# Reading the FFN weights earlier: absolute sums in the QKV stage, quantisation in the attention stage

## The chip, the cores and the metric

The kernel runs on all 8 cores of one Trainium2 chip. Each core computes one of the 8 sequences by itself and holds its own copy of the weights in device memory; the cores exchange nothing. The metric is device microseconds (us) of the slowest core.

## The reference

One transformer layer on `x` of shape (8, 4096, 1024), float32: `x = x + Attn(LN(x))`, then `x = x + FFN(LN(x))`. LN has no gain or bias.

```python
# attention, one head, d_k = 128, causal
Q, K, V = x @ Wq, x @ Wk, x @ Wv
attn = softmax(mask(Q @ K.T * 128 ** -0.5)); out = (attn @ V) @ Wo
# FFN, 1024 -> 4096 -> 1024, weights and activations quantised
def _weight_quant(w):
    scale = 1.0 / clip(mean(abs(w)), 1e-05)
    return clip(round(w * scale), -1.0, 1.0) / scale
def _act_quant(x):
    scale = 127.0 / clip(max(abs(x), axis=-1), 1e-05)
    return clip(round(x * scale), -128.0, 127.0) / scale
gate = silu(_act_quant(x) @ wq(w_gate).T); up = _act_quant(x) @ wq(w_up).T
y = _act_quant(gate * up) @ wq(w_down).T
```

What matters here is `_weight_quant`: each of the three 16 MB weight matrices needs the mean of its absolute values before a single element can be quantised. So each matrix is read from memory twice: pass 1 sums the absolute values, pass 2 multiplies by the scale, clips, rounds and stores bf16.

## The kernel before

The program is written out by hand as five instruction lists, one an engine, with explicit semaphores. `sc.op(engine, fn, waits, inc)` appends an instruction to the list of TensorE ('t'), VectorE ('v'), ScalarE ('s'), GpSimd ('g') or SyncE ('q'). Nothing reorders them later: each engine works through its list in the order in which the Python code emitted it, and an instruction that waits holds all that stand behind it. A DMA is an instruction of the engine that issues it ('q' and 'g' for loads, 's' for most stores).

The 4096 rows of `x` are NT = 32 tiles of 128 rows. The stages follow one another:

1. **QKV stage** (`emit_p1_A`, `emit_p1_B`, `emit_p1_geo`). Per tile: load x into one half of `x2_st` (named x_st in the profile; two buffers), DVE sums the rows (L234), ACT squares and sums them (L239), a chain of small DVE instructions and one ACT Sqrt (L254) give mean and 1/sigma, ACT normalises into `nqh_sb[:, 0:1024]` (L261), PE transposes, DVE copies, PE makes Q, K and V, DVE and ACT evict them (L294, L296, L298). On each engine the sum and the square of tile i+1 are emitted ahead of the rest of tile i; the x load of tile i+2 waits for L261 of tile i.
2. **Attention stage** (`emit_pa1_group`), 8 groups g of 4 query tiles. PE computes scores (L479), ACT takes the exponential (L490 to L497), PE multiplies by V (L454), DVE inverts the row sums (L516), ACT scales the output (L522) and stores it (L527). After each group **pass 1** of the weights follows: four pieces of 128x2048 of w_gate or w_up and four of 128x1024 of w_down (`emit_w1_piece`). A piece is a load (L206) and an ACT Abs with a running sum (L210). Each kind of piece has two buffers: `x2_st` and `wstage` for the wide ones, loaded by SP, `nqh_sb` and `nqt_sb` for the narrow ones, loaded by POOL. `emit_scales` follows the last group: for each of the three matrices a chain of small DVE and PE instructions (L320 to L339).
3. **Wo stage**, 8 groups of 4 tiles. Per group the attention output comes back (L575), PE transposes it, DVE copies it (L594). Per tile: PE multiplies by Wo (L632, L635), DVE adds x (L641, L643) in one of four x buffers (loaded at L430 into the two halves of `x2_st` and of `wstage`), ACT issues the store of x1 (L647), and one tile later the statistics of the second LN follow (`emit_stats`: DVE L604, ACT L609, DVE L613 to L619). The load of tile i+4 waits for statistics and store of tile i. Between the add and the statistics stands **pass 2**: one wide and one narrow piece per tile (`emit_w2_piece`). A piece is a load (L379), two DVE instructions (L382, L385) and one ACT instruction (L388 into the resident `wgq` or `wuq`; L395 into the single buffer `wdq_st`, which ACT then stores to memory, L397). Two buffers per kind: parts of `qres` and `kres`, free since attention is over, for the wide pieces, `nqh_sb` and `nqt_sb` for the narrow ones.
4. **FFN stage**: per tile the quantised activations times `wgq` and `wuq` (L790, L797), silu, product, quantisation.
5. **Down stage**: per tile the product with the quantised w_down (L936).

The two rules that bind a piece of pass 2 for w_down are in these lines: the buffer's next load waits for the ACT instruction, and the ACT instruction waits for the store before it.

```python
            if idx >= 33:
                wds.append(('DSW', ds_wdq[idx - 1]))
            s_qdone[idx] = sc.op('s', (lambda dstap=dstap: (lambda e: e.activation(
                wdq_st, dstap, AF.Identity, bias=ng_c)))(), waits=wds, inc='S')
```

## Time and profile before

| what | us |
|---|---|
| median of 2 runs | 2870.09 (2844.27 and 2895.91) |
| the profiled execution | 2851.59 |
| its span, slowest core (core 4) | 2850.0 |
| spans of the eight cores | 2828.4 to 2850.0 |
| QKV stage, to the first score matmul | 0 to 335.9 |
| attention stage with pass 1 | 335.9 to 646.3 |
| Wo stage with pass 2 | 646.3 to 1046.3 |
| FFN stage | 1046.3 to 2362.4 |
| down stage | 2362.4 to 2850.0 |

The span is the time from the first to the last instruction of the profiled execution; the execution's own time is 1.6 us longer. In the rows below PE is TensorE's matmul, PEld its weight load, DVE VectorE, ACT ScalarE, POOL GpSimd, SP SyncE; an engine's name with a q (ACTq, SPq) is its sequencer issuing a DMA. PEclk is TensorE's granted clock as a share of 2.4 GHz. "DMA share" is the mean busy share of the core's 16 DMA engines. Buffer numbers are left out of names.

### The profile page before, as it was taken

How to read it: one execution, taken by the hardware profiler on the slowest of the kernel's cores; microseconds unless marked ns; L12 is line 12 of the kernel's file. 1: busy time of each engine (PE TensorE's matmuls, PEld its weight loads, DVE VectorE, ACT ScalarE, POOL GpSimd, SP SyncE). 2: the span in 40 equal slices, each digit the busy share in tenths (PEclk: the TensorE clock that was granted, in tenths of full speed). 3: DMA queues.
4: the chain of work that ended last, by engine and by line, in shares of the span. 5: the costliest groups of instructions: out<-in, count | busy, mean ns of one | idle time of the engine just before them, and what ended most of it. 6: DMA issues, size and time to landing. Idle time of an engine off the chain costs nothing.

```text
span 2850.0 us, 25295 instructions; the slowest of 8 cores (2828.4 to 2850.0 us)
## 1 busy us (share of the span) xinstructions
PE 1692.4 (59%) x9479; PEld 881.7 (31%) x9618; DVE 912.1 (32%) x1481; ACT 866.0 (30%) x829; POOL 95.1 (3%) x168
## 2 busy tenths in 40 slices
PE   2333313330001017877777787778777875999999
PEld 2333212230000003333333333334333432444444
DVE  2333200004556554334434433443444331000110
ACT  2322355562333333333333333333333331000000
POOL 1000011011111100000000000000000000000000
PEclk9855556665555559999999999999999997999999
DMA  3111354446777740100110011001001006444443
GB/s 68 52 52 55 102 183 152 162 139 227 244 242 233 241 161 30 45 30 37 45 45 30 38 45 45 30 37 45 37 32 44 37 15 211 158 148 148 148 156 125
DMA packets 69993, 290.07 MB, mean 102 GB/s; under 512 B 10352, under 2 KB 12400, under 8 KB 53488
## 3 DMA queue, kind: packets, MB, share of 16 engines
q1 hardware_dynamic: 28592, 143.73, 15.8%
q0 software_dynamic: 21696, 68.17, 7.8%
q10 hardware_dynamic: 19584, 76.55, 6.6%
q8 instruction: 77, 1.26, 0.2%
q14 instruction: 44, 0.36, 0.0%
HBM read 212.93 MB, written 76.55 MB: 102 GB/s over the span
## 4 chain that ended last, share of the span: by engine, by line
PE 55%; DMA 13%; DVE 12%; ACT 9%; issue 8%; DVEq 1%; POOL 1%; ACTq 0%; SPq 0%; POOLq 0%
PE pb L797 17%; PE pb L790 16%; PE pb L936 16%; DMA nqt_sb<-wdt 4%; DMA nqh_sb<-wdt 4%; DVE h_sb L809 3%; ACT kres L807 3%; DMA wstage<-wgt 1%; ACT nqh_sb L261 1%; DVE st_cols L814 1%; DVE st_cols L234 1%; ACT wdq_st L395 1%; DMA wdqh<-wdq_st 1%; PE pb L274 1%; PE pb L283 1%
## 5 line engine op out<-in xcount | busy, mean ns | idle before, releaser
L790 PE MATMUL pb<-wgq,qres 128*128 128x512 bf16 x1952 | 770.7, 395 | 254.5 <-DVE qres L773 251.7
L797 PE MATMUL pb<-wuq,qres 128*128 128x512 bf16 x2048 | 806.2, 394 | 43.0 <-DVE h_sb L809 38.1
L936 PE MATMUL pb<-wdq_sb,nqt_in 128*128 128x512 bf16 x2007 | 442.1, 380 | 25.0 <-DMA nqt_in<-nqh 22.6
L809 DVE SCALAR_TENSOR_TENSOR h_sb<-pb,st_cols,kres 128x1024 f32<-128x1024 f32 x128 | 164.3, 1284 | 736.4 <-ACT kres L807 736.4
L790 PEld LDWEIGHTS pb<-wgq,qres 128*128 128x128 bf16 x2048 | 206.9, 101 | 551.2 <-issue 332.0
L807 ACT ACTIVATE kres<-pb,st_cols 128x1024 f32<-128x1024 f32 x128 | 142.5, 1113 | 495.6 <-PE pb L797 333.5
L797 PEld LDWEIGHTS pb<-wuq,qres 128*128 128x128 bf16 x2048 | 205.6, 100 | 253.3 <-issue 33.6
L936 PEld LDWEIGHTS pb<-wdq_sb,nqt_in 128*128 128x128 bf16 x2048 | 200.8, 98 | 266.0 <-issue 25.9
L632 PE MATMUL pb<-wo_sb,ot_sb 128*128 128x512 bf16 x30 | 18.1, 603 | 319.8 <-DVE ot_sb L594 319.8
L867 ACT ACTIVATE nqh_sb<-h_sb,konst 128x4096 bf16<-128x4096 f32 x32 | 118.7, 3708 | 215.1 <-DVE h_sb L865 215.1
L479 PE MATMUL pb<-qres,kres 128*128 128x128 bf16 x528 | 52.4, 260 | 189.0 <-ACT pt L497 174.3
L946 DVE SCALAR_TENSOR_TENSOR out_sb<-pb,c_all,x_in 128x512 f32<-128x512 f32 x32 | 24.0, 750 | 431.2 <-PE pb L936 431.2
L814 DVE TENSOR_REDUCE st_cols<-h_sb 128x1 f32<-128x1024 f32 x128 | 156.1, 1220 | 11.7
L274 PE MATMUL pb<-ident_sb,nqh_sb 128*128 128x128 bf16 x256 | 32.4, 306 | 184.9 <-ACT nqh_sb L261 184.9
L632 PEld LDWEIGHTS pb<-wo_sb,ot_sb 128*128 128x128 bf16 x32 | 4.1, 127 | 332.6 <-issue 332.6
L479 PEld LDWEIGHTS pb<-qres,kres 128*128 128x128 bf16 x528 | 42.1, 119 | 195.1 <-issue 192.5
L516 DVE RECIPROCAL rq_sb<-pb 128x1 f32<-128x1 f32 x32 | 2.9, 154 | 284.9 <-PE pb L454 284.9
L274 PEld LDWEIGHTS pb<-ident_sb,nqh_sb 128*128 128x128 bf16 x256 | 24.8, 137 | 192.3 <-issue 192.3
L865 DVE TENSOR_SCALAR h_sb<-h_sb,st_cols,konst 128x4096 f32<-128x4096 f32 x32 | 77.2, 2411 | 5.3 <-DVE c_all L863 5.3
L739 ACT ACTIVATE qres<-ln_scr,konst 128x1024 bf16<-128x1024 f32 x32 | 36.7, 1148 | 130.4 <-DVE ln_scr L732 130.4
L839 ACT ACTIVATE nqt_sb<-pb 128x2048 bf16<-128x2048 bf16 x31 | 58.2, 1877 | 21.1 <-PE pb L832 21.1
L497 ACT ACTIVATE pt<-pb,konst 128x1024 bf16<-128x1024 f32 x56 | 59.0, 1112 | 7.4 <-PE pb L479 4.5
(147 smaller groups left out, 1556.1 us busy)
## 6 DMA issues: line engine op xcount, KB each, us to landing
nqh<-nqt_sb ACTq DMA_DIRECT2D x32, 1024.0 KB, 3.9
nqt_in<-nqh SPq DMA_DIRECT2D x32, 1024.0 KB, 5.2
x_st<-x POOLq DMA_DIRECT2D x48, 512.0 KB, 4.6
nqh_sb<-wdt POOLq DMA_DIRECT2D x32, 512.0 KB, 7.3
nqt_sb<-wdt POOLq DMA_DIRECT2D x32, 512.0 KB, 7.4
x_st<-x1h SPq DMA_DIRECT2D x32, 512.0 KB, 3.3
x_in<-x1h SPq DMA_DIRECT2D x32, 512.0 KB, 6.8
y<-out_sb ACTq DMA_DIRECT2D x32, 512.0 KB, 7.0
```

Source lines behind the costliest of these rows:

```text
L274: tt = sc.op('t', (lambda c=c, par=par: (lambda e: e.transpose(psA[par][:, c * 128:(c + 1) * 128], ln1_sb[:, c * 128:(c + 1) * 128], ident ...
L479: tt = sc.op('t', (lambda k=k, q=q, pbst=pbst, off=off, j=j: (lambda e: e.matmul(pbst[:, off + j * 128: off + (j + 1) * 128], kres[:, k * ...
L497: s_exp_last[pp] = sc.op('s', (lambda pp=pp, ptx=ptx: (lambda e: e.activation(pt_row[ptx][:, 0:1024], pb[pp][:, 0:1024], AF.Exp, scale=sms ...
L790: tt = sc.op('t', (lambda c=c, o0=o0, gb=gb, half=half, par=par: (lambda e: e.matmul(gb[:, half * 512:(half + 1) * 512], xqTb[par][:, c * ...
L797: tt = sc.op('t', (lambda c=c, o0=o0, ub=ub, half=half, par=par: (lambda e: e.matmul(ub[:, half * 512:(half + 1) * 512], xqTb[par][:, c * ...
L807: s_silu_q[(i, qtr)] = sc.op('s', (lambda gb=gb, i=i: (lambda e: e.activation(g_s, gb, AF.Silu, scale=c1g_p[i % 2])))(), waits=sw, inc='S')
L809: v_stt_q[(i, qtr)] = sc.op('v', (lambda qtr=qtr, ub=ub, i=i: (lambda e: e.scalar_tensor_tensor(h_sb[:, qtr * 1024:(qtr + 1) * 1024], ub, ...
L814: sc.op('v', (lambda qtr=qtr: (lambda e: e.reduce_max(mh4[:, qtr:qtr + 1], h_sb[:, qtr * 1024:(qtr + 1) * 1024], axis=AX, apply_absolute_v ...
L839: ss2 = sc.op('s', (lambda fg=fg: (lambda e: e.activation(nqt_sb[:, 0:2048], fg.bitcast(BF16)[:, 0:2048], AF.Identity)))(), waits=sw2, inc ...
L865: vv = sc.op('v', lambda e: e.tensor_scalar(h_sb, h_sb, s2q_c, cb_c, ALU.mult, ALU.add), waits=[('V', v_stt_q[(i, 3)])], inc='V')
L867: s_nqh_t[i] = sc.op('s', lambda e: e.activation(nqh_sb, h_sb, AF.Identity, bias=ng_c), waits=[('V', vv)], inc='S')
L936: tt = sc.op('t', (lambda c=c, half=half, par=par: (lambda e: e.matmul(dps[par][:, half * 512:(half + 1) * 512], nqt_in[par][:, c * 128:(c ...
```

## The change

Both passes over the weights move one stage ahead.

- Pass 1 goes into the QKV stage: after each tile three pieces are emitted, 96 in all. All pieces are now 128x1024, all are loaded by SP, and they go through four buffers: the two halves of `wstage` and the columns 1024 to 3072 (bf16) of `nqh_sb` and `nqt_sb`, which the QKV stage does not use. The first four loads wait for nothing.
- `emit_scales` stands between the QKV stage and attention, and the first scores wait for it.
- Pass 2 goes into the attention stage: after each of the 8 groups eight pieces are emitted, the 32 wide ones of w_gate and w_up after groups 0 to 3, the 32 of w_down after groups 4 to 7. All are loaded by SP, through four buffers of 128x2048: `x2_st`, `wstage`, `nqh_sb`, `nqt_sb`.
- The Wo stage has no weight work left. Its first x loads wait for the last ACT instruction of pass 2 and for its store to memory.

```diff
-    w1stages = [x2_st, wst2]
+    w1stages = [wst2[:, 0:1024], wst2[:, 1024:2048],
+                nqh_sb.bitcast(F32)[:, 512:1536], nqt_sb.bitcast(F32)[:, 512:1536]]
+    w2stages = [x2_st, wst2,
+                nqh_sb.bitcast(F32)[:, 0:2048], nqt_sb.bitcast(F32)[:, 0:2048]]
...
     def emit_w1_piece(idx):
         wi, src, wid = wpieces[idx]
...
+        par = idx % 4
+        dstap = w1stages[par][:, 0:wid]
+        w = [('S', s_abs[idx - 4])] if idx >= 4 else []
+        v = sc.op('q', (lambda src=src, dstap=dstap: (lambda e: e.dma_start(out=dstap, in_=src)))(),
+                  waits=w, inc='DQW%d' % par, n=16)
...
     for i in range(NT):
         if i + 1 < NT:
             emit_p1_A(i + 1)
         s_ln1x = emit_p1_B(i)
         emit_p1_geo(i, s_ln1x)
+        for _ in range(3):
+            if w1_next < len(wpieces):
+                emit_w1_piece(w1_next)
+                w1_next += 1
...
     def emit_w2_piece(idx):
         wi, src, dst, wid = p2pieces[idx]
         s_col = wsc[:, 2 * wi:2 * wi + 1]
...
+        par = idx % 4
+        dstap = w2stages[par][:, 0:wid]
+        if idx < 4:
+            w = [('S', s_abs[-1]), ('T', p1_T), ('V', p1_V), ('S', s_lastx[NT - 1])]
         else:
...
+            w = [('S', s_qdone[idx - 4])]
+        v = sc.op('q', (lambda src=src, dstap=dstap: (lambda e: e.dma_start(out=dstap, in_=src)))(),
+                  waits=w, inc=w2sems[par], n=16)
...
     def emit_xload_pa(i):
...
-            w = [('S', s_abs[-1])]
+            w = [('S', s_qdone[-1] if s_qdone[-1] else 0), ds_wd_done]
...
+    emit_scales()
+    w2_next = 0
     for g in range(NT // GRP):
         emit_pa1_group(g)
-        for _ in range(4):
-            if w1_next < 32:
-                emit_w1_piece(w1_next)
-                w1_next += 1
...
-    emit_scales()
+        for _ in range(8):
+            if w2_next < len(p2pieces):
+                emit_w2_piece(w2_next)
+                w2_next += 1
...
             ds_x1[i] = ('DSX%d' % pari, v)
-            if w2_next[0] < 32:
-                emit_w2_piece(w2_next[0])
-                w2_next[0] += 1
-            if wd2_next[0] < 64:
-                emit_w2_piece(wd2_next[0])
-                wd2_next[0] += 1
             if j >= 1:
                 emit_stats(i - 1)
```

Line numbers shift: of the changed kernel L198 is the Abs (before L210), L227 the square (L239), L242 the Sqrt (L254), L249 the normalisation (L261), L284 the eviction of K (L296), L373 and L380 the ACT instruction of pass 2 (L388, L395), L382 its store (L397), L624 the store of x1 (L647), L586 the square of the second LN (L609).

ACT's list in the QKV stage, before, from the Sqrt of one tile to the Sqrt of the next (x2_st is the profile's x_st):

```order
L254 ACTIVATE st_cols<-st_cols,konst 128x1
L261 ACTIVATE nqh_sb<-x2_st,st_cols 128x1024
L296 ACTIVATE kres<-pb1 128x128
L239 ACTIVATE ln_scr,st_cols<-x2_st 128x1024
L254 ACTIVATE st_cols<-st_cols,konst 128x1
```

The same place in the changed kernel:

```order
L242 ACTIVATE st_cols<-st_cols,konst 128x1
L249 ACTIVATE nqh_sb<-x2_st,st_cols 128x1024
L284 ACTIVATE kres<-pb1 128x128
L198 ACTIVATE wstage0,wsums<-wstage0 128x1024 x2
L198 ACTIVATE nqh_sb,wsums<-nqh_sb 128x1024
L227 ACTIVATE ln_scr,st_cols<-x2_st 128x1024
L242 ACTIVATE st_cols<-st_cols,konst 128x1
```

Three Abs instructions (two halves of wstage, then nqh_sb) now stand between the eviction of K and the square of the tile after next, and so ahead of the Sqrt of the next tile.

ACT's list behind an attention group, before (group 0; L522 scales the output, L527 stores it, L497 is the first exponential of group 1):

```order
L522 ACTIVATE pt2<-pb3,rq_sb 128x128 x2
L527 DMA oh<-pt2 128x512
L210 ACTIVATE x2_st,wsums<-x2_st 128x2048
L210 ACTIVATE wstage0,wsums<-wstage0 128x2048
L210 ACTIVATE x2_st,wsums<-x2_st 128x2048
L210 ACTIVATE wstage0,wsums<-wstage0 128x2048
L210 ACTIVATE nqh_sb,wsums<-nqh_sb 128x1024
L210 ACTIVATE nqt_sb,wsums<-nqt_sb 128x1024
L210 ACTIVATE nqh_sb,wsums<-nqh_sb 128x1024
L210 ACTIVATE nqt_sb,wsums<-nqt_sb 128x1024
L497 ACTIVATE pt0<-pb0,konst 128x1024
```

In the changed kernel, behind group 7 (with pieces of w_down; behind groups 0 to 3 eight rows of L373 stand there instead), from its fifth piece on into the Wo stage:

```order
L380 ACTIVATE wdq_st<-x2_st,konst 128x1024
L382 DMA wdqh<-wdq_st 128x1024
L380 ACTIVATE wdq_st<-wstage0,konst 128x1024
L382 DMA wdqh<-wdq_st 128x1024
L380 ACTIVATE wdq_st<-nqh_sb,konst 128x1024
L382 DMA wdqh<-wdq_st 128x1024
L380 ACTIVATE wdq_st<-nqt_sb,konst 128x1024
L382 DMA wdqh<-wdq_st 128x1024
L624 DMA x1h<-x2_st 128x1024 x2
L586 ACTIVATE ln_scr,st_cols<-x2_st 128x1024
L624 DMA x1h<-wstage0 128x1024
L586 ACTIVATE vres,wsums<-x2_st 128x1024
```

The weight work stays in one block behind each group, ahead of the next group's exponentials; in the Wo stage ACT now has only the stores of x1 and the squares.

## Rows read from the trace of the kernel before

**Rows 1.** Busy time of attention and Wo stage: each engine, clock, DMA share, GB/s.

```profile
335.90:646.30 310.40, 89.10 (x1068) 80.42 (x1068) 4.47 (x44) 180.84 (x249) 29.57 (x64) 0.60 0.51 166
646.30:1046.30 400.00, 32.32 (x100) 11.71 (x102) 226.01 (x334) 136.29 (x130) 45.06 (x64) 0.52 0.71 234
```

**Rows 2.** Timeline of ACT, one QKV tile: start, length, instruction, idle before.

```profile
127.81 0.28 ACT L296 ACTIVATE kres<-pb 128x128 bf16<-128x128 f32 x1 [4.91 <-PE pb L291]
128.09 1.06 ACT L239 ACTIVATE ln_scr<-x_st 128x1024 f32<-128x1024 f32 x1
...
130.60 0.29 ACT L254 ACTIVATE st_cols<-st_cols,konst 128x1 f32<-128x1 f32 x1 [1.35 <-DVE st_cols L251]
...
137.71 0.28 ACT L296 ACTIVATE kres<-pb 128x128 bf16<-128x128 f32 x1 [4.91 <-PE pb L291]
```

**Rows 3.** Timeline of ACT, attention group 1's end, weight block, next exponential.

```profile
377.01 1.14 ACT L522 ACTIVATE pt<-pb,rq_sb 128x128 bf16<-128x128 f32 x4 [2.21 <-DVE rq_sb L516]
...
391.77 1.04 ACT L210 ACTIVATE nqh_sb<-nqh_sb 128x1024 f32<-128x1024 f32 x1
...
392.81 1.04 ACT L210 ACTIVATE nqt_sb<-nqt_sb 128x1024 f32<-128x1024 f32 x1
...
403.03 2.10 ACT L497 ACTIVATE pt<-pb,konst 128x1024 bf16<-128x1024 f32 x2
```

**Rows 4.** Chain that ended last, a tile of the Wo stage: start, length, what.

```profile
991.90 6.79 DMA nqt_sb<-wdt
...
1000.55 1.16 ACT wdq_st L395
```

**Rows 5.** From issue to landing by line, us: L169, L430, L647, L397.

```profile
DMA to landing us min/median/max: 4.4/4.6/12.9
DMA to landing us min/median/max: 3.7/5.4/8.8
DMA to landing us min/median/max: 2.9/6.5/9.2
DMA to landing us min/median/max: 2.0/2.8/7.0
```

**Rows 6.** Timeline, the third scale after pass 1 to the first add.

```profile
646.41 0.19 DVE L320 TENSOR_REDUCE st_cols<-wsums 128x1 f32<-128x32 f32 x1 [6.00 <-ACT nqt_sb L210]
...
648.96 0.15 DVE L339 COPY wscales<-pb 128x1 f32<-128x1 f32 x1
...
658.48 0.42 DVE L594 COPY ot_sb<-pb 128x512 bf16<-128x512 bf16 x1 [9.38 <-PE pb L589]
...
660.24 0.69 DVE L641 TENSOR_TENSOR x_st<-pb,x_st 128x512 f32<-128x512 f32 x1 [1.33 <-PE pb L635]
```

**Rows 7.** Timeline, a wide piece and a narrow one of pass 2 on DVE, ACT.

```profile
665.44 1.29 DVE L382 TENSOR_SCALAR qres<-qres,wscales 128x2048 f32<-128x2048 f32 x1 [3.92 <-DMA qres<-wgt]
...
668.03 0.75 DVE L382 TENSOR_SCALAR nqh_sb<-nqh_sb,wscales 128x1024 f32<-128x1024 f32 x1
668.21 2.00 ACT L388 ACTIVATE wgq<-qres,konst 128x2048 bf16<-128x2048 f32 x1 [21.90 <-DVE qres L385]
```

**Rows 8.** Busy time: a stretch with full DMA engines, and the first 17 us.

```profile
650.00:656.00 6.00, 0.00 (x0) 0.00 (x0) 0.00 (x0) 0.00 (x0) 0.00 (x0) 0.50 1.00 333
...
0.00:17.00 17.00, 0.00 (x0) 0.00 (x0) 1.01 (x11) 0.00 (x0) 4.62 (x10) 1.00 0.78 123
```

**Rows 9.** Timeline of the Wo stage: store issue, square, next add, next store issue.

```profile
678.86 0.33 ACTq L397 DMA_DIRECT2D wdqh<-wdq_st  x1
679.23 1.06 ACT L609 ACTIVATE ln_scr<-x_st 128x1024 f32<-128x1024 f32 x1 [0.45 <-ACT wdq_st L395]
...
680.65 0.69 DVE L641 TENSOR_TENSOR wstage<-pb,wstage 128x512 f32<-128x512 f32 x1
...
682.02 0.33 ACTq L647 DMA_DIRECT2D x1h<-wstage  x1
```

**Rows 10.** Groups of instructions by line: a load of ACT's tables.

```profile
L490 ACT ACT_TABLE_LOAD x1 | 1.3, 1283 | 1.6 <-PE pb L479 1.6
```

More of the change, by code:

```diff
@@ L175, in _build @@
         for c in range(HC):
-            for hh in range(2):
-                wpieces.append((wi, wd_ap[c * 128:(c + 1) * 128, hh * 2048:(hh + 1) * 2048], 2048))
+            for hh in range(4):
+                wpieces.append((wi, wd_ap[c * 128:(c + 1) * 128, hh * 1024:(hh + 1) * 1024], 1024))
     for p in range(OC):
@@ L182, in _build @@
     s_abs = [0] * len(wpieces)
[L183 to L185 removed]
+    w1stages = [wst2[:, 0:1024], wst2[:, 1024:2048],
+                nqh_sb.bitcast(F32)[:, 512:1536], nqt_sb.bitcast(F32)[:, 512:1536]]
+    w2stages = [x2_st, wst2,
+                nqh_sb.bitcast(F32)[:, 0:2048], nqt_sb.bitcast(F32)[:, 0:2048]]
+    w2sems = ['DQW0', 'DQW1', 'DQW2', 'DQW3']
     def emit_w1_piece(idx):
         wi, src, wid = wpieces[idx]
[L189 to L208 removed]
+        par = idx % 4
[3 more added lines that the diff above has]
+                  waits=w, inc='DQW%d' % par, n=16)
+        dq_p1w[idx] = ('DQW%d' % par, v)
         col = wsums[:, idx:idx + 1]
@@ L304, in _build @@
     emit_p1_A(0)
+    w1_next = 0
     for i in range(NT):
@@ L309, in _build @@
         emit_p1_geo(i, s_ln1x)
+        for _ in range(3):
+            if w1_next < len(wpieces):
+                emit_w1_piece(w1_next)
+                w1_next += 1
+    while w1_next < len(wpieces):
+        emit_w1_piece(w1_next)
+        w1_next += 1
     v_vones = sc.op('v', lambda e: e.memset(vres[:, 128::129], 1.0), inc='V')
@@ L323, in emit_scales @@
                 pb[0][0:1, 0:1], tot_col, ones_c, start=True, stop=True)))(),
-                waits=[('V', vv), ('S', s_exp_last[0]), ('S', s_exp_last[1])], inc='T')
+                waits=[('V', vv), ('V', v_evA[0]), ('V', v_evA[1])], inc='T')
             vv = sc.op('v', lambda e: e.tensor_scalar(tot_sb[:, 0:1], pb[0][0:1, 0:1], INV_WN, EPS, ALU.mult, ALU.max),
@@ L331, in emit_scales @@
             tt = sc.op('t', lambda e: e.matmul(pb[1][0:128, 0:1], ones_r, tot_sb[:, 1:2], start=True, stop=True),
-                       waits=[('V', vv), ('S', s_exp_last[2] if False else 0)], inc='T')
+                       waits=[('V', vv), ('V', v_evQ[0]), ('S', s_evK[0])], inc='T')
             tt = sc.op('t', lambda e: e.matmul(pb[1][0:128, 512:513], ones_r, tot_sb[:, 2:3], start=True, stop=True),
@@ L361, in emit_w2_piece @@
         s_col = wsc[:, 2 * wi:2 * wi + 1]
[L362 to L381 removed]
+        par = idx % 4
+        dstap = w2stages[par][:, 0:wid]
+        if idx < 4:
+            w = [('S', s_abs[-1]), ('T', p1_T), ('V', p1_V), ('S', s_lastx[NT - 1])]
+        else:
+            w = [('S', s_qdone[idx - 4])]
+        v = sc.op('q', (lambda src=src, dstap=dstap: (lambda e: e.dma_start(out=dstap, in_=src)))(),
+                  waits=w, inc=w2sems[par], n=16)
+        vw = [(w2sems[par], v), ('V', v_konst), ('V', v_scale_done[0])]
         v_q = sc.op('v', (lambda dstap=dstap, s_col=s_col: (lambda e: e.tensor_scalar(
@@ L529, in emit_pa1_group @@
         dso_g[g] = dso_last[0]
-    w1_next = 0
-    wd1_next = 32
+    emit_scales()
+    w2_next = 0
     for g in range(NT // GRP):
         emit_pa1_group(g)
-        for _ in range(4):
-            if w1_next < 32:
-                emit_w1_piece(w1_next)
-                w1_next += 1
-        for _ in range(4):
-            if wd1_next < 64:
-                emit_w1_piece(wd1_next)
-                wd1_next += 1
-    while w1_next < 32:
-        emit_w1_piece(w1_next)
-        w1_next += 1
-    while wd1_next < 64:
-        emit_w1_piece(wd1_next)
-        wd1_next += 1
-    emit_scales()
+        for _ in range(8):
+            if w2_next < len(p2pieces):
+                emit_w2_piece(w2_next)
+                w2_next += 1
+    while w2_next < len(p2pieces):
+        emit_w2_piece(w2_next)
+        w2_next += 1
+    s_wq_done = s_qdone[31]
+    ds_wd_done = ('DSW', ds_wdq[-1])
     t_attn_pt[0] = sc.cnt['T']
-    w2_next = [0]
-    wd2_next = [32]
     emit_xload_pa(0)
@@ L659, in _build @@
         emit_stats(g0 + GRP - 1)
-    while w2_next[0] < 32:
-        emit_w2_piece(w2_next[0])
-        w2_next[0] += 1
-    while wd2_next[0] < 64:
-        emit_w2_piece(wd2_next[0])
-        wd2_next[0] += 1
-    s_wq_done = s_qdone[31]
-    ds_wd_done = ('DSW', ds_wdq[-1])
     ss = sc.op('s', lambda e: e.activation(var_all, var_all, AF.Sqrt, bias=eps_c),
```

47 lines of the change are left out of this document (3 added, 44 removed).

## The prediction

> **What bounds the kernel now.** I read the busy time by stage first, then the chain that ended last, then the timeline inside one repetition of each stage that the change touches. The FFN and the down stage keep their instructions and their order, so the question is what the 1046.3 us ahead of them become.
>
> QKV stage: one tile takes 9.9 us, from one eviction of K to the next (127.81 to 137.71) [rows 2]. It is a loop of latencies through all engines: behind the eviction comes DVE's sum of the tile after, then its small instructions, and ACT's Sqrt starts 2.79 us after the eviction (130.60); normalisation, transposes, copy and projections fill the other 7.1 us. ACT is idle for most of it: 1.35 us ahead of the Sqrt, 4.91 us ahead of the eviction.
>
> Attention stage: DMA share 0.51, ACT 181 of 310 us [rows 1]. Behind each group stands a block of weight pieces: the scaled output of group 1 is done at 378.15 and the next exponential starts at 403.03 [rows 3], 25 us in which nothing of attention moves. There are eight such blocks, some 200 of the 310 us; attention proper takes 110.
>
> Wo stage: 400 us for 32 tiles, no engine above 226 us, DMA at 234 GB/s and a share of 0.71 [rows 1]. The chain says why: the load of one narrow w_down piece (6.79 us), its two DVE instructions, its ACT instruction, then the next load into the freed buffer [rows 4]. Latency holds it, not an engine: from the first add at 660.24 [rows 6] to the last statistics (1046.2, the stage's end) it takes 386 us, 12 a tile.
>
> **The change part by part.** The same work is done twice (the same bytes are read, summed and quantised), so all that counts is what each piece stands beside.
>
> *Start.* Four loads of 0.52 MB, 2.1 MB in all, now run while the first x tile loads. Alone that is 6.3 us at the full 333 GB/s; in the first 17 us the DMA engines are busy 78% and so have 3.7 us free [rows 8]. Bounds 2.6 and 6.3 us; I take +4.
>
> *QKV stage.* Three Abs now follow each eviction of K. An Abs of 128x1024 whose data is there comes every 1.04 us (391.77 to 392.81) [rows 3]. The Sqrt of the next tile then starts after 0.28 + 3 x 1.04 + 1.07 (the square, 1.06 long [rows 2]) = 4.5 us instead of 2.79. That is +1.7 a tile. If each Abs takes as long as a square up to the instruction that waits for it, 1.42 us (679.23 to 680.65) [rows 9], it is +2.8. I take 1.9, near the row of the Abs itself: 31 x 1.9 = +59 (53 to 87). The tile becomes 11.8 us long. In it move 4 x 0.52 MB = 2.1 MB, 178 GB/s, against 333 with full engines [rows 8]. The three loads are issued behind the Abs and are over within about 5 to 7 us, an Abs asks for them only a tile later; so the loads themselves are hidden. SP's queue holds nothing else here; POOL's keeps only the x loads, since w_down leaves it.
>
> *Scales.* Three chains of 2.7 us (646.41 to 649.11) [rows 6] now stand between the last tile and the first scores, 8.1 us; before, 0.9 us of the gap was there anyway and the loads of the next stage hid the third. +8 (7 to 8). Behind the waiting scores stands only attention on PE, and behind it ACT's exponentials.
>
> *Blocks 0 to 3 (wide pieces).* DVE needs 2.6 us for a wide piece (665.44 to 668.03), ACT 2.00 behind it [rows 7]. Eight pieces make 21 us on DVE. Four pieces are loaded while the group's attention runs; the fifth is issued when ACT has done the first, about 4.8 us into the block, and needs some 6.8 us (as the load in [rows 4]), so DVE waits 1 to 3 us in the middle. With the last ACT instruction, and less the 1.5 us in which ACT still scales the output, a block is 24.5 us (22.5 to 28) against 25: 4 x -0.5 = -2.
>
> *Blocks 4 to 7 (narrow pieces).* Here `wdq_st` is one buffer: each ACT instruction waits for the store of the one before it. 1.16 us [rows 4], 0.1 to issue, 2.8 to land (median of L397, in a stage more loaded than this one) [rows 5], 0.2 for semaphores: 4.25 us. Seven of these, one last instruction and the start: 31.4 us against 25, 4 x 6.4 = +26. In the Wo stage this wait was mostly covered by other waits; here nothing covers it. With a landing of 2.0 us the four blocks lose 3 us, with twice the median, 5.6, they lose 104.
>
> *Entry to the Wo stage.* Before, 13.8 us from the last Abs to the first add (646.4 to 660.24) [rows 6], held by a load of attention output behind six others. Now the last store must land (2.8), then an x load (5.4) [rows 5]; with issue some 9.5. -4.
>
> *Wo stage.* With the pieces gone, three limits are close. The loop of add and statistics: a store issue at 678.86, the square, the next add at 680.65, its store issue at 682.02 [rows 9], so 3.16 us a tile; once in a group the copy of the attention output and two matmuls, 1.76 us (658.48 to 660.24) [rows 6], and one statistics more: 3.5 us a tile on average. The transfers: 1.05 MB a tile and 0.13 MB a group, 3.2 us at 333 GB/s [rows 8], 4.6 us at this stage's present 234 [rows 1]. The four x buffers: load 5.4, add 1.4, store 6.5 [rows 5], issues 0.5, 13.8 us for four tiles, 3.4 a tile (5.0 with the longest landings). None lies under another, so they will get in each other's way; I take 4.2 (3.5 to 5.0): 32 x 4.2 = 134 instead of 386, -252.
>
> The Trainium skill ("HBM Reference", Specifications (TRN2)) gives each of two streaming cores about 358 GB/s. At that rate 1.08 MB takes 3.0 us, an estimate, and only the loop of add and statistics would be left, 3.5 us a tile and 2668 in all, the first rival's time. The trace has 333 GB/s at a share of 1.00, a little under it [rows 8].
>
> *FFN and down stage.* Their first instructions wait for the same statistics and for x1 tiles stored long before. 0 (up to +1).
>
> Sum: 4 + 59 + 8 - 2 + 26 - 4 - 252 = -161. Against the profiled execution's own 2851.6 us that is 2690. That execution lies 0.6% under the median of the two runs shown, 2870; one of them lies at 2844, beside it, so I count from the profiled one.
>
> **The rivals.**
>
> *The Wo stage stops only at its loop* (3.5 us a tile, 112 us): 2668. For it: the loop is the longest of the three limits at the rate of full engines. Against: the transfers then need 310 GB/s without a break, and landings at 234 GB/s already take 5.4 and 6.5 us.
>
> *The store of w_down holds blocks 4 to 7.* If loads of 0.52 MB in the same blocks push the landing to 5.6 us, 28 x 2.8 = +78 on the forecast: 2768. For it: the longest in the trace is 7.0 [rows 5]. Against: its median is 2.8 under 234 GB/s, and the blocks will run at about 0.79 MB in 4.3 us, 185 GB/s.
>
> *ACT changes its tables in the QKV stage.* Sqrt and Abs now alternate. If no set of tables holds both, each tile pays two loads of 1.283 us [rows 10], 32 x 2.57 = +82: 2772. The trace shows Abs beside exponentials at no load, and Square and Identity beside Sqrt; it never shows Abs beside Sqrt. The Trainium skill ("ScalarE: Activation LUTs", Table sets: the hidden batching unit) says that abs is in every set; by that there is no load, and the Abs between exponentials agree.
>
> *Slower: x comes late in the QKV stage.* x is loaded by POOL, one tile at a time behind L261, while SP holds up to four weight loads. Before, x lands 4.6 us after its issue [rows 5], just in time. After, it may take about 6.7 us, since DVE's sum has 1.7 to 2.3 us of room. From there each us costs 31. If the weight loads stand in front of it and it takes 12.9 us, as the longest of this line did, that is 6.2 x 31 = +192: 2882, slower by 1%; over 2% slower from 13.7 us on. Against: the weight loads of a tile are issued 3.5 to 5.5 us ahead of x's issue and are done when it comes; and the 12.9 us were the first loads, behind the four attention weights.
>
> **How the numbers follow.** Forecast, about 2690 with its own range 2650 to 2735: 0.66. Loop alone: 0.12. Store: 0.10. Tables: 0.04. x late: 0.05. The rest, several small terms together between 2740 and 2830: 0.03. All terms at their low ends give about 2630, all at their high ends some 2840. The range that should hold it 8 times in 10 is 2650 to 2765: a tenth is left above, a tenth below. 2% (about what a measurement of this kernel can tell from no change) is 57 us; faster by more than that, under 2795, takes all cases but x late and the end of the rest: 0.92. Within 2%: 0.05. Slower: 0.03.
>
> **What would show it.** Right: K's evictions 11.6 to 12.3 us apart; ACT_TABLE_LOAD still four in all; the first score at about 407; weight blocks of about 24 us after groups 0 to 3 and 31 after 4 to 7, in which L380 waits for the DMA wdqh<-wdq_st; the Wo stage from about 750 to 890; FFN and down stage as long as before. The forecast is wrong if the Wo stage stays above 6 us a tile, if blocks 4 to 7 exceed 40 us, or if L227 or DVE's sum of x waits for x tile after tile.

## The result, and the profile after

The changed kernel takes 2719.5 us (median of 9 runs, 2716.9 to 2802.9) against 2855.7 for the kernel before (median of 8, 2844.3 to 2895.9). The ratio of the two is 0.9535 with an interval of 0.9521 to 0.9549, so it is faster by 4.5% to 4.8%. In the longest run of the nine, 2802.9 us, the cores of one die had a granted clock of 0.77 to 0.78 instead of 0.81; the ratios, here and below, leave such runs out. Forecast was 2690 in a range of 2650 to 2765: the direction and the range hold, and the kernel is 30 us slower than the forecast. The profiled execution of the changed kernel took 2719.5 us with a span of 2718.0 (core 5), where that of before had a span of 2850.0: -132, where the sum of the prediction said -161.

I read the changed profile in the same order as before: the stages, then the inside of one repetition of each.

Busy time by stage of the changed kernel: start:end and length, PE, PEld, DVE, ACT, POOL (instructions), granted clock, DMA share, GB/s. The rows are QKV, attention and Wo stage; the second and the third answer to [rows 1].

```profile
0.00:398.00 398.00, 122.84 (x1042) 107.23 (x1042) 108.92 (x316) 188.96 (x353) 20.48 (x40) 0.59 0.63 175
398.00:771.00 373.00, 86.06 (x1056) 77.70 (x1056) 130.42 (x162) 182.39 (x184) 12.60 (x32) 0.59 0.50 156
771.00:914.00 143.00, 31.73 (x96) 10.53 (x96) 99.37 (x203) 38.70 (x68) 16.95 (x32) 0.57 0.74 246
```

The Wo stage has shrunk from 400 us to 143, and attention has grown from 310 to 373: it has the same ACT work as before (182 us) and the same DMA share (0.50), but is 63 us longer. That growth is what the forecast missed most of.

The QKV stage, as the timeline of ACT from one eviction of K to the next (start, length, instruction, idle before it):

```profile
207.74 0.28 ACT L284 ACTIVATE kres<-pb 128x128 bf16<-128x128 f32 x1 [4.91 <-PE pb L279]
207.92 1.05 ACT L198 ACTIVATE wstage<-wstage 128x1024 f32<-128x1024 f32 x1
...
211.03 1.04 ACT L227 ACTIVATE ln_scr<-x_st 128x1024 f32<-128x1024 f32 x1
212.07 0.28 ACT L242 ACTIVATE st_cols<-st_cols,konst 128x1 f32<-128x1 f32 x1
219.18 0.28 ACT L284 ACTIVATE kres<-pb 128x128 bf16<-128x128 f32 x1 [4.91 <-PE pb L279]
```

A tile takes 11.4 us instead of 9.9 [rows 2]. The three Abs (the first is shown) and the square behind them come every 1.04 us, and the Sqrt of the next tile starts 4.33 us after the eviction instead of 2.79. ACT waits 4.91 us ahead of the eviction, to the hundredth what it waited before: the loop has only been made longer at the place where the Abs were put in.

The start and the first load of ACT's tables, from the groups of instructions (busy time and mean ns | idle time before, and what ended it):

```profile
L227 ACT ACT_TABLE_LOAD x1 | 1.3, 1283 | 24.5 <-DMA x_st<-x 24.5
```

It is one of four such groups, of one load each (the others are at L475, L632 and L770), as many as before. So an Abs between two Sqrt costs none. The first x tile lands at 24.5 us where it landed at 17.1 before.

Timeline of ACT in the attention stage: first the wide block behind group 0, then the narrow block behind group 4 and the exponential behind it, then the last narrow pieces behind group 7 (ACTq is an issue of a DMA by ACT):

```profile
406.06 0.35 ACTq L512 DMA_DIRECT2D oh<-pt  x1
...
431.30 2.10 ACT L482 ACTIVATE pt<-pb,konst 128x1024 bf16<-128x1024 f32 x2
...
552.12 0.33 ACTq L512 DMA_DIRECT2D oh<-pt  x1
552.55 1.15 ACT L380 ACTIVATE wdq_st<-x_st,konst 128x1024 bf16<-128x1024 f32 x1 [0.51 <-DVE x_st L370]
558.78 1.15 ACT L380 ACTIVATE wdq_st<-wstage,konst 128x1024 bf16<-128x1024 f32 x1 [5.08 <-DMA wdqh<-wdq_st]
564.51 1.15 ACT L380 ACTIVATE wdq_st<-nqh_sb,konst 128x1024 bf16<-128x1024 f32 x1 [4.59 <-DMA wdqh<-wdq_st]
...
595.38 2.12 ACT L482 ACTIVATE pt<-pb,konst 128x1024 bf16<-128x1024 f32 x2 [0.79 <-ACT wdq_st L380]
...
766.58 1.15 ACT L380 ACTIVATE wdq_st<-wstage,konst 128x1024 bf16<-128x1024 f32 x1 [2.19 <-DMA wdqh<-wdq_st]
769.91 1.15 ACT L380 ACTIVATE wdq_st<-nqh_sb,konst 128x1024 bf16<-128x1024 f32 x1 [2.18 <-DMA wdqh<-wdq_st]
773.25 1.15 ACT L380 ACTIVATE wdq_st<-nqt_sb,konst 128x1024 bf16<-128x1024 f32 x1 [2.19 <-DMA wdqh<-wdq_st]
```

The wide block runs from 406.06 to 431.30, 25.2 us, much like one of before (378.15 to 403.03 [rows 3]). The narrow one runs from 552.12 to 595.38, 43.3 us. Its instructions are 5.7 us apart and each is released by the store of the one before. Only the last four of the stage, for which no load is left to issue, are 3.3 us apart.

What was issued beside those stores shows in the timeline of SP, ACT and DVE in the same block:

```profile
565.73 0.33 SPq L364 DMA_DIRECT2D nqh_sb<-wdt  x1
565.74 0.36 ACTq L382 DMA_DIRECT2D wdqh<-wdq_st  x1
570.08 0.75 DVE L367 TENSOR_SCALAR nqh_sb<-nqh_sb,wscales 128x1024 f32<-128x1024 f32 x1 [4.13 <-DMA nqh_sb<-wdt]
```

The ACT instruction that ends at 565.7 releases two transfers at once: the store of what it wrote, and the load into the buffer that it has read. Both land some 4.4 us later.

The waits of that line (engine, tile, line, what released it: sum of us, count, longest), and the time from issue to landing of its store:

```profile
ACT wdq_st L380 <- DMA wdqh<-wdq_st: 124.4, 28, 5.1
...
DMA to landing us min/median/max: 2.0/4.5/4.9
```

The median landing is 4.5 us, where it was 2.8 in the Wo stage of before [rows 5], and the lowest, 2.0, is the same.

The entry and the Wo stage, from the timeline of DVE: the first add; the four adds of the second group of tiles and the first of the third; and the last statistics:

```profile
783.36 0.69 DVE L618 TENSOR_TENSOR x_st<-pb,x_st 128x512 f32<-128x512 f32 x1 [4.68 <-DMA x_st<-x]
...
800.03 0.69 DVE L618 TENSOR_TENSOR x_st<-pb,x_st 128x512 f32<-128x512 f32 x1 [1.33 <-PE pb L612]
...
801.24 0.68 DVE L618 TENSOR_TENSOR x_st<-pb,x_st 128x512 f32<-128x512 f32 x1
...
804.73 0.69 DVE L618 TENSOR_TENSOR wstage<-pb,wstage 128x512 f32<-128x512 f32 x1
...
808.24 0.69 DVE L618 TENSOR_TENSOR wstage<-pb,wstage 128x512 f32<-128x512 f32 x1
...
815.70 0.69 DVE L618 TENSOR_TENSOR x_st<-pb,x_st 128x512 f32<-128x512 f32 x1 [1.33 <-PE pb L612]
...
911.11 0.21 DVE L596 TENSOR_SCALAR var_all<-wsums 128x1 f32<-128x1 f32 x1 [0.16 <-issue]
```

From the last piece's ACT instruction (774.4) to the first add it takes 9.0 us instead of 13.8 [rows 6]. From there to the last statistics it is 128 us, 4.0 a tile. Inside a group two adds with one statistics between them are 3.5 us apart (804.73 to 808.24). A whole group of four takes 15.67 us (800.03 to 815.70), since two statistics, the copy of the attention output and two matmuls stand between its last add and the next group's first. That is 3.92 us a tile, and in this group nothing waits for x: four of the seven steps from group to group take exactly as long. So 3.92 of the 4.0 us are the loop itself. x tiles that come late add some 4 us in the whole stage (steps of 16.67, 16.32 and 18.29 us); the chain that ended last has three such loads behind the entry, this the longest (start, length, what):

```profile
880.91 8.49 DMA wstage<-x
```

So the account is this: -258 us in the Wo stage and -5 at the entry, against some +130 elsewhere, most of it in the QKV stage (+47) and in the blocks behind groups 4 to 7 (+69). What I wanted to know from the chip was where that cost comes from, and which half of the change earns anything.

### The profile page after: what moved, and what is told of

Read it like the earlier page. It is cut to its first block, busy times and chain, and to the rows that moved or that the text cites. A ratio compares the mean times of both kernels' runs of the same rounds, so it can differ in the third digit from the quotient of the medians.

```text
span 2718.0 us, 25663 instructions; the slowest of 8 cores (2698.5 to 2718.0 us)
## 1 busy us (share of the span) xinstructions
PE 1707.6 (63%) x9618; PEld 881.4 (32%) x9618; DVE 912.8 (34%) x1481; ACT 862.2 (32%) x893; POOL 50.0 (2%) x104
## 4 chain that ended last, share of the span: by engine, by line
PE 56%; DMA 12%; ACT 11%; DVE 11%; issue 7%; DVEq 2%; POOL 1%; ACTq 0%; POOLq 0%; SPq 0%
PE pb L753 18%; PE pb L760 17%; PE pb L899 16%; DMA x_st<-x 5%; DMA wdqh<-wdq_st 5%; DVE h_sb L772 3%; ACT kres L770 3%; ACT nqh_sb L249 1%; DVE st_cols L777 1%; ACT wdq_st L380 1%; PE pb L464 1%; ACT wstage L198 1%; ACT ln_scr L227 1%; PE pb L439 1%; DVEq L369 1%
## 5 line engine op out<-in xcount | busy, mean ns | idle before, releaser
L753 PE MATMUL pb<-wgq,qres 128*128 128x512 bf16 x2048 | 808.4, 395 | 286.6 <-DVE qres L736 252.4
L770 ACT ACTIVATE kres<-pb,st_cols 128x1024 f32<-128x1024 f32 x128 | 142.7, 1115 | 496.9 <-PE pb L760 334.8
L899 PEld LDWEIGHTS pb<-wdq_sb,nqt_in 128*128 128x128 bf16 x2048 | 200.9, 98 | 265.5 <-issue 25.5
L262 PE MATMUL pb<-ident_sb,nqh_sb 128*128 128x128 bf16 x256 | 32.4, 307 | 239.7 <-ACT nqh_sb L249 239.7
L262 PEld LDWEIGHTS pb<-ident_sb,nqh_sb 128*128 128x128 bf16 x256 | 24.8, 138 | 247.1 <-issue 247.1
L609 PE MATMUL pb<-wo_sb,ot_sb 128*128 128x512 bf16 x32 | 19.1, 598 | 90.5 <-DVE ot_sb L571 87.0
L795 PE MATMUL pb<-ident_sb,nqh_sb 128*128 128x128 bf16 x992 | 60.4, 219 | 0.0
L795 PEld LDWEIGHTS pb<-ident_sb,nqh_sb 128*128 128x128 bf16 x992 | 58.0, 98 | 7.3
```

The lines of the kernel that those rows point to most:

```text
L753: tt = sc.op('t', (lambda c=c, o0=o0, gb=gb, half=half, par=par: (lambda e: e.matmul(gb[:, half * 512:(half + 1) * 512], xqTb[par][:, c * ...
L770: s_silu_q[(i, qtr)] = sc.op('s', (lambda gb=gb, i=i: (lambda e: e.activation(g_s, gb, AF.Silu, scale=c1g_p[i % 2])))(), waits=sw, inc='S')
L795: tt2 = sc.op('t', (lambda c=c, pbx=pbx, coff=coff: (lambda e: e.transpose(pbx.bitcast(BF16)[:, coff:coff + 128], nqh_sb[:, c * 128:(c + 1 ...
L899: tt = sc.op('t', (lambda c=c, half=half, par=par: (lambda e: e.matmul(dps[par][:, half * 512:(half + 1) * 512], nqt_in[par][:, c * 128:(c ...
```

## The experiments

I took three theories to the chip. *A (store and load)*: a narrow piece costs 5.7 us because the store of 0.26 MB is issued in the same instant as a load of 0.52 MB and they share the DMA engines; ACT waits for it because there is one `wdq_st`. Its rival *B* is that the block is bound by something else: the transfers' volume, DVE, or the load itself. *A (place of the Abs)*: an Abs costs time only because it stands between the eviction and the Sqrt, and none in ACT's gap ahead of the eviction. Its rival is that any Abs, or its load, costs the loop the same wherever it stands. *A (start)*: the late first x tile comes from the four early loads. Where I compare two of my kernels I give the difference of their medians, since the ratios are all to the kernel before. The kernel before has itself medians of 2855.7, 2851.0 and 2846.8 us in the three sets of measurements, so such a difference is good to some 9 us.

**Pass 1 alone.** Pass 1 stays in the QKV stage as in the change; pass 2 goes back to the Wo stage, with the buffers and queues of before.

```diff
     for g in range(NT // GRP):
         emit_pa1_group(g)
-        for _ in range(8):
-            if w2_next < len(p2pieces):
-                emit_w2_piece(w2_next)
-                w2_next += 1
...
             ds_x1[i] = ('DSX%d' % pari, v)
+            if w2_next[0] < 32:
+                emit_w2_piece(w2_next[0])
+                w2_next[0] += 1
+            if wd2_next[0] < 64:
+                emit_w2_piece(wd2_next[0])
+                wd2_next[0] += 1
```

> Only pass 1 is moved (into the QKV stage); pass 2 stays in the Wo stage with the buffers and queues of the kernel before. Theory A, moving pass 2 gained nothing, since its eight blocks hold attention 266 us in the changed kernel and the Wo stage became only 258 us shorter: first score at 398, attention 110 us, entry about 10, Wo stage 386 as before, span about 2712, so 4.5 to 5.2% under before, like the changed kernel within 0.5%. Theory B, the gain comes from the Wo stage freed of pass 2, as the forecast's largest term has it: without it the kernel is near the one before, above 2790.

Measured: ratio 0.9545 (0.9481 to 0.9609), beside 0.9535 (0.9521 to 0.9549) for the whole change; profiled span 2719.8 beside 2718.0. Moving pass 2 moved no time that can be told. Busy time by stage of this kernel, attention and Wo stage:

```profile
400.00:516.00 116.00, 82.21 (x1056) 73.70 (x1056) 2.91 (x32) 82.83 (x121) 12.61 (x32) 0.82 0.03 9
516.00:914.60 398.60, 30.97 (x94) 10.53 (x96) 225.06 (x328) 136.05 (x129) 46.30 (x64) 0.53 0.71 235
```

Attention without any block takes 116 us with the DMA engines all but idle (0.03), and the Wo stage is back at 399, as in [rows 1]. Together that is 515 us; in the changed kernel the same two stages take 373 + 143 = 516. So the 256 us that leave the Wo stage come back in the blocks and in the end of attention. What makes the change faster is pass 1 alone, which goes from blocks of 25 us into a stage where the three Abs of a tile, 3.1 us of ACT, make the tile only 1.5 us longer.

**Four buffers for the stores.** `wdq_st` becomes four buffers (three in columns that attention leaves free), each with its own semaphore.

```diff
+    wdq4 = [wdq_st, nqh_sb[:, 2048:3072], nqh_sb[:, 3072:4096], nqt_sb[:, 2048:3072]]
+    wdq4sem = ['DSW', 'DSW_1', 'DSW_2', 'DSW_3']
...
-            if idx >= 33:
-                wds.append(('DSW', ds_wdq[idx - 1]))
+            bf = idx % 4
+            if idx >= 36:
+                wds.append((wdq4sem[bf], ds_wdq[idx - 4]))
```

> The changed kernel with four buffers for the quantised w_down piece instead of one, each with its own semaphore. Theory A, the single buffer holds blocks 4 to 7 (an ACT instruction every 5.8 us, 4.6 of it waiting for the store): blocks 4 to 7 fall from 43 us to the pace of the loads, 20 to 26 us, the last from 35 to about 22, so 65 to 85 us less than the changed kernel, span about 2640. Theory B, the loads of w_down hold these blocks and the store only hides them: each piece still takes 5 us or more, the blocks stay above 38 us, gain under 20 us.

Measured: 2624.0 us, ratio 0.9189 (0.9126 to 0.9252), 95 us under the changed kernel, more than expected. Timeline of ACT in block 4, and the busy time of the same stretch:

```profile
554.42 1.15 ACT L383 ACTIVATE wdq_st<-x_st,konst 128x1024 bf16<-128x1024 f32 x1 [0.51 <-DVE x_st L372]
556.11 1.15 ACT L383 ACTIVATE nqh_sb<-wstage,konst 128x1024 bf16<-128x1024 f32 x1 [0.54 <-DVE wstage L372]
...
562.76 1.15 ACT L383 ACTIVATE wdq_st<-x_st,konst 128x1024 bf16<-128x1024 f32 x1 [2.12 <-DVE x_st L372]
...
571.57 2.12 ACT L485 ACTIVATE pt<-pb,konst 128x1024 bf16<-128x1024 f32 x2 [0.54 <-ACT nqt_sb L383]
```

```profile
554.00:571.50 17.50, 1.12 (x16) 0.91 (x16) 10.45 (x15) 9.20 (x8) 0.00 (x0) 0.53 0.84 263
```

The block takes 17.2 us from its first ACT instruction to the next exponential (42.8 in the changed kernel, 552.55 to 595.38). The same bytes move in 40% of the time, at 263 GB/s and a share of 0.84. That rules out the volume, DVE and the load as what bound the block; the wait for the one buffer did. Now ACT waits for DVE, which waits for its loads. A single store lands even later here, 6.3 us after its issue at the median, and no ACT instruction waits for one.

**The Abs in ACT's gap.** The three pieces of a tile are emitted between the two halves of the tile's own work, ahead of the eviction of K and not behind it.

```diff
         s_ln1x = emit_p1_B(i)
-        emit_p1_geo(i, s_ln1x)
         for _ in range(3):
             if w1_next < len(wpieces):
                 emit_w1_piece(w1_next)
                 w1_next += 1
+        emit_p1_geo(i, s_ln1x)
```

> The changed kernel, with the three Abs of a tile emitted ahead of the eviction of K instead of behind it, where ACT waits 4.9 us for PE. Theory A, only their place in ACT's list costs, not their loads: K's evictions come 9.9 to 10.1 us apart instead of 11.4, the QKV stage is 43 to 48 us shorter, span about 2672. Theory B, the weight loads (2.1 MB in 9.9 us with x, 212 GB/s) delay x: DVE's sum or the Abs wait for loads, tiles stay at 11 us or more, gain under 15 us.

Measured: 2669.0 us, ratio 0.9340 (0.9286 to 0.9395), 50.5 us under the changed kernel. Timeline of ACT, one QKV tile of this kernel:

```profile
156.22 1.04 ACT L198 ACTIVATE nqh_sb<-nqh_sb 128x1024 f32<-128x1024 f32 x1
...
159.15 0.28 ACT L284 ACTIVATE kres<-pb 128x128 bf16<-128x128 f32 x1 [1.80 <-PE pb L279]
...
161.92 0.29 ACT L242 ACTIVATE st_cols<-st_cols,konst 128x1 f32<-128x1 f32 x1 [1.24 <-DVE st_cols L239]
...
169.03 0.28 ACT L284 ACTIVATE kres<-pb 128x128 bf16<-128x128 f32 x1 [1.80 <-PE pb L279]
```

The tile is back at 9.88 us (159.15 to 169.03), the Sqrt starts 2.77 us after the eviction, and the idle time ahead of the eviction has fallen from 4.91 to 1.80 us: the three Abs, 3.1 us, now stand in it. From the first square to the last eviction of K the stage takes 320.2 us here, 365.4 in the changed kernel and 318.0 in the kernel before: 45 of the 47 us came from the place. The other 2 us are a few longer tiles, some of which wait for x.

**The first weight loads wait for x.** The first four loads of pass 1 wait for the first two x tiles.

```diff
-        w = [('S', s_abs[idx - 4])] if idx >= 4 else []
+        w = [('S', s_abs[idx - 4])] if idx >= 4 else [dg_x[0], dg_x[1]]
```

> The changed kernel, whose first four weight loads wait until the first two x tiles have landed. Theory A, the four loads at the start take the DMA engines from x: the first square starts near 17 us again instead of 24.5, span 7 us shorter, 0.25%, nothing later since the first Abs comes 11 us after. Theory B, x is late for another reason (its queue, the attention weights): the start stays at 24 us and the time does not change.

Measured: 2711.1 us, ratio 0.9489 (0.9440 to 0.9538). Its interval overlaps that of the changed kernel, so by time alone this is not told apart; the trace does it. Timeline of the slowest core:

```profile
19.63 1.28 ACT L227 ACT_TABLE_LOAD   x1 [19.63 <-DMA x_st<-x]
20.90 0.80 SPq L194 DMA_DIRECT2D wstage<-wgt  x2
```

Over the eight cores this first load of the tables stands at 16.4 to 19.7 us. In the changed kernel it stands at 23.5 to 27.1, in the kernel before at 16.9 to 18.2. The four early loads did it.

**The load behind the store.** Same one buffer, but a load of a narrow piece also waits until the store of four pieces ago, the one that had just been issued, has landed. A load now starts when that store has landed, with the next ACT instruction and so 1.2 us ahead of the next store, and later than before. Volume and buffers are unchanged.

```diff
             w = [('S', s_qdone[idx - 4])]
+            if idx >= 36:
+                w.append(('DSW', ds_wdq[idx - 4]))
```

> The changed kernel with one more wait: the load into a stage buffer of w_down also waits for the store of the piece that was in it, so that load and store are no longer issued in the same instant (in the changed kernel SP's load and ACT's store both wait for the same ACT instruction and are issued 0.01 us apart). Theory A, the store lands late (4.5 us instead of 2.0) because the load is issued with it and takes the DMA engines: now the load's bytes fall beside the ACT instruction and only in part beside the next store, whose landing falls to 2.5 to 3.5 us; an ACT instruction every 3.9 to 4.8 us instead of 5.8, blocks 4 to 6 about 30 to 36 us instead of 43, span 2675 to 2700. Theory B, any load in flight costs the store the same: cycle still 5.5 us or more, span 2715 or more.

Measured once: 2679.3 us, 40 us under the changed kernel although it only adds a wait. Timeline of ACT in block 4, and the landing of the store:

```profile
575.24 1.15 ACT L382 ACTIVATE wdq_st<-wstage,konst 128x1024 bf16<-128x1024 f32 x1 [3.14 <-DMA wdqh<-wdq_st]
580.06 1.15 ACT L382 ACTIVATE wdq_st<-nqh_sb,konst 128x1024 bf16<-128x1024 f32 x1 [3.67 <-DMA wdqh<-wdq_st]
```

```profile
DMA to landing us min/median/max: 2.0/3.1/4.1
```

The median landing falls from 4.5 to 3.1 us and behind the block's first step of 3.3 us the pieces are 4.3 to 4.9 us apart (the one after the two shown stands at 584.60). Of the 2.5 us that a store needs beyond the 2.0 of one alone, 1.4 are gone once the load starts 1.2 us ahead of it; the rest stays while a load is in flight.

**Half the narrow loads left out.** In each of blocks 4 to 7 only the first four pieces load their data; the last four work on what lies in the buffer, so half of w_down is not read in pass 2. A piece without a load waits as its load would.

```diff
+        if idx < 36 or idx % 8 < 4:
+            v = sc.op('q', (lambda src=src, dstap=dstap: (lambda e: e.dma_start(out=dstap, in_=src)))(),
+                      waits=w, inc=w2sems[par], n=16)
+            w2land[par] = v
+        v = w2land[par]
+        vw = [(w2sems[par], v), *w, ('V', v_konst), ('V', v_scale_done[0])]
```

> The changed kernel without the loads of every second four pieces of w_down (the last four pieces of each of blocks 4 to 7 are quantised from what lies in the buffers; half of w_down is left out of the result). In each of blocks 4 to 6 the first four stores then go without a load, the last four with one. Theory A, the load issued with the store makes it late: the first four ACT instructions come 3.3 us apart, the last ones 5.8 us, blocks 4 to 6 about 33 us instead of 43, block 7 about 26, span about 2680. Theory B, stores are late in blocks 4 to 6 for another reason than the loads (the last four of block 7 were fast because it is the end): 5.8 us throughout, span near 2718.

Measured once: 2697.8 us, where I expected about 2680. Six cores have spans of 2664.9 to 2676.1, but cores 4 and 5 take 2696.1 and 2692.0, and the slowest sets the time. Their 20 us are not lost in the blocks: between 1000 and 1600 us, in the FFN stage, these two have a granted clock of 0.87 and some 2360 weight loads of PE done, where the others have 0.91 to 0.92 and 2456 to 2482. The other six are near the expected 2680. Timeline of ACT on core 1, block 4:

```profile
562.26 1.15 ACT L385 ACTIVATE wdq_st<-nqh_sb,konst 128x1024 bf16<-128x1024 f32 x1 [2.20 <-DMA wdqh<-wdq_st]
565.60 1.15 ACT L385 ACTIVATE wdq_st<-nqt_sb,konst 128x1024 bf16<-128x1024 f32 x1 [2.19 <-DMA wdqh<-wdq_st]
568.95 1.15 ACT L385 ACTIVATE wdq_st<-x_st,konst 128x1024 bf16<-128x1024 f32 x1 [2.19 <-DMA wdqh<-wdq_st]
574.69 1.15 ACT L385 ACTIVATE wdq_st<-wstage,konst 128x1024 bf16<-128x1024 f32 x1 [4.59 <-DMA wdqh<-wdq_st]
```

Inside one block the step between pieces is 3.3 us where no load goes out with the store, and 5.7 to 5.9 where one does. The four pieces of 3.3 at the end of the changed kernel are no oddity of the stage's end. With the two runs before it this settles the store: the load beside it adds 2.4 us, one buffer makes ACT wait for that.

**The three edits together**: four store buffers, the Abs in the gap, the first loads behind x.

> The changed kernel with four store buffers, the Abs ahead of K's eviction, and the first four weight loads behind the first two x tiles. Theory A, the three act on different stages and add up: against the changed kernel -94, -49 and -7 us, span near 2568, 0.90 of the kernel before. Theory B, they compete for the DMA engines and part of the gain is lost: over 2590.

Measured: 2566.7 us, ratio 0.9012 (0.8999 to 0.9026), 153 us under the changed kernel, where the three single differences sum to 95 + 50.5 + 8.4 = 154. That is agreement within the 9 us. In the trace two of them do meet: against the run with the Abs in the gap alone the first square comes 7.3 us earlier (19.5 against 26.8), but from there to the last eviction of K it takes 325.9 us instead of 320.2, with early tiles of up to 13 us. What is left of attention is shown below beside the next kernel.

**A piece after each pair of key tiles.** On top of the three edits the pieces leave the blocks: one is emitted inside each group behind the matmuls with V of a pair, so that it stands between two exponentials of ACT.

```diff
                 emit_av(pend.pop(0))
+            if w2_next[0] < len(p2pieces):
+                emit_w2_piece(w2_next[0])
+                w2_next[0] += 1
...
     for g in range(NT // GRP):
         emit_pa1_group(g)
-        for _ in range(8):
-            if w2_next < len(p2pieces):
-                emit_w2_piece(w2_next)
-                w2_next += 1
```

> As e7, and the 64 pieces of pass 2 are no longer emitted in blocks of eight behind each group but one behind each pair of key tiles, between the exponentials. Theory A, the blocks cost attention because ACT and PE stand still while DVE and DMA work: spread out, the loads (58 MB at 290 to 333 GB/s, 175 to 200 us) run beside attention proper (110 us); attention stage 230 to 280 us instead of about 290, span 2510 to 2560. Theory B, each exponential then waits for a piece and its load, so that nothing overlaps: attention stage stays at 290 us or grows, span 2570 or more.

Measured: 2512.0 us, ratio 0.8822 (0.8808 to 0.8837), faster than before and than the change. Busy time of the attention stage, first of the three edits together, then of this kernel, and below them ACT's timeline of this kernel:

```profile
353.40:626.00 272.60, 86.10 (x1056) 77.86 (x1056) 130.08 (x160) 183.64 (x185) 12.62 (x32) 0.62 0.60 213
```

```profile
351.40:566.00 214.60, 120.96 (x1056) 103.17 (x1056) 131.59 (x160) 178.87 (x185) 19.08 (x36) 0.52 0.81 271
```

```profile
424.50 1.99 ACT L375 ACTIVATE wuq<-x_st,konst 128x2048 bf16<-128x2048 f32 x1
426.39 1.11 ACT L485 ACTIVATE pt<-pb,konst 128x1024 bf16<-128x1024 f32 x1
427.39 2.00 ACT L375 ACTIVATE wuq<-wstage,konst 128x2048 bf16<-128x2048 f32 x1
```

In this group weights and exponentials alternate on ACT without a gap. The stage is now near two limits together, ACT (179 of 215 us) and the DMA engines (share 0.81, 271 GB/s). PE's granted clock is 0.52, near the lower of its two levels (1.2 GHz), and PE's busy time has risen from 86 to 121 us, which I take to cost nothing, since ACT and the transfers take longer; no run here isolates it.

## Why the prediction was right, and where it was wrong

By its own terms, from the profiled executions:

- *Start*, +4 forecast, **+7.4** measured (24.5 against 17.1), beyond the upper bound of 6.3. That bound was the four loads' transfer at full rate, 6.3 us, so x is delayed by the whole of it and a little more. I had subtracted the idle share of the DMA engines in the first 17 us; it did not help x. That the loads are the cause is shown by the run in which they wait for x.
- *QKV stage*, +59 forecast (53 to 87), **+47** measured: 1.53 us a tile instead of 1.9. The step was right (Abs every 1.04 us, on the way from eviction to Sqrt), its size wrong: I put all four instructions behind the eviction in a row with their full lengths, and took +1.7 up to 1.9 for the unknown. The Sqrt in fact starts 4.33 us after the eviction, not 4.5, since in the row each begins a little before the end of the one ahead of it. The upper bound rested on a misread row: the instruction that waits for that square is at 680.48, 1.25 us behind its start, not the add at 680.65. The run with the Abs in the gap shows the reason right.
- *Scales*, +8 forecast, **+7.6** measured (last eviction at 389.91, first score at 398.43, 8.5 us instead of 0.9).
- *Blocks 0 to 3*, -2 forecast, **-4** measured: 25.3, 24.8, 24.9 and 25.5 us, against 104.5 for the four of before. I forecast 24.5 each against 25.
- *Blocks 4 to 7*, +26 forecast, **+69** measured: 43.3, 43.0, 43.7 and 35.4 us, 165.4 together against 96.2. **This is the term that failed.** The mechanism was named (one `wdq_st`, each ACT instruction behind the last store), and its cycle was laid out as 1.16 + 0.1 + landing + 0.2. What failed is the landing of 2.8 us, taken as the median of L397 "in a stage more loaded than this one". Load in that sense, GB/s over a stage, was the wrong measure. In the Wo stage of before a load went out within 1 us of only two of the 32 stores, and the next narrow load mostly 3 to 6 us behind the store, since POOL held it behind an x load; here the store goes out in the same instant as a load of twice its size, every time. Measured: 4.5 us in place of 2.8, a cycle of 5.7 in place of 4.25. The three runs on store and load show it from three sides. The prediction had named blocks over 40 us as a sign that it is wrong, and by that sign this part of it is.
- *Entry*, -4 forecast, **-4.8** measured.
- *Wo stage*, -252 forecast, **-258** measured: 4.0 us a tile where I took 4.2. The size is right by luck. I had the loop at 3.5 us and added 0.7 for loads, stores and loop getting in each other's way; measured, the loop is 3.92 and late x tiles add some 0.13. The loop came out too short because I read the store issue at 678.86 as one of x1: it is L397, the store of w_down, and DVE's sum of that tile had been done before it (675.06). So 3.16 us was no full turn; a turn takes 3.5.
- *FFN and down stage*, 0 forecast, **+2.9** measured. The first x1 tile's load on the chain explains 1.1 (4.36 us against 3.24); the rest I did not look into.

The terms measured sum to -133 (the spans differ by 132), 28 above the forecast: +43 from blocks 4 to 7, and -15 from all the others. Those -15, of which -12 are the Abs step that was priced too high, hide a third of the miss in the sum.

Of the rivals, *the store of w_down holds blocks 4 to 7* came nearest in its mechanism. I had given it a tenth and priced it with a landing of 5.6 us; with 4.5 it is 28 x 1.7 = +48, at 2738, of which other terms gave some back. *The Wo stage stops only at its loop* was nearly right in its mechanism, with 3.92 of 4.0 us a tile, and wrong in its price: at 3.92 instead of 3.5 its time is 2681, not 2668. By the rate in the Trainium skill ("HBM Reference", Specifications (TRN2)) that loop would have been the only limit, and the trace agrees but for some 4 us of late x tiles; the stage moved 246 GB/s at a share of 0.74. The tables did not change, as the Trainium skill ("ScalarE: Activation LUTs", Table sets: the hidden batching unit) has it for abs, and the four loads in the profile agree. x did not come late in the QKV stage in a way that mattered: the profile has waits of DVE for it, but the run with the Abs in the gap reached the old period of 9.9 us in most tiles with the same loads.

What the prediction never asked is which half of the change earns. The sum had -252 for pass 2's leaving and took its blocks for granted, since blocks had stood there before. Put per half, the same rows would have said that pass 1 leaves 200 us of blocks and costs some 60 + 8 + 4 in QKV, while pass 2 trades 256 us of Wo stage and entry for 8 new blocks, four of 24.5 and four of 31.4 us by my own terms, 224 in all. I would then have seen that this half earns some 30 us, and that those hang on the one estimate with the least behind it.

## What to carry to other kernels

A piece that is moved costs what the place makes of it: the same three Abs cost 1.5 us a tile behind an eviction and next to nothing in the idle time ahead of it, and the 64 pieces of pass 2 lengthen attention by 1.5 us each between the exponentials (214.6 us against 116 without any). With the same four store buffers they cost 2.4 us each in blocks (272.6 us), and with one buffer a narrow one in a block costs 5.7. Look for the idle time in the row of the engine that carries it, and move the piece into it, one at a time, not into a block.
When one instruction releases a store and a load together and something waits for the store through a single buffer, price the store with the load beside it, or give it a second buffer. And split a change into its halves before summing: a large gain and a large loss that cancel look like part of a success.
